# A two-layer graph convolution with residual and layer norm: unrolled chunks, pairs of 1024 nodes, layer 2 in node layout, row statistics two at a time

## What is computed

```python
def conv(x, src, dst, ea, W_msg, W_edge, W_root, b):
    msg = x[src] @ W_msg + ea @ W_edge
    agg = segment_max(msg, dst, num_segments=N)      # -inf becomes 0
    return agg + x @ W_root + b
c1 = leaky_relu(conv(x,  ..., W1_msg, W1_edge, W1_root, b1))
c2 = leaky_relu(conv(c1, ..., W2_msg, W2_edge, W2_root, b2))
out = layernorm(x + c2)                              # over the 96 features, eps 1e-5
```

## Time and profile before

| | us |
|---|---|
| median of 3 runs | 1723.3 (1714.0 to 1755.0) |
| span of the profiled execution | 1697.5 |
| its PE, DVE, ACT, POOL busy | 979, 1044, 667, 1056 |
| its stage A, to the last scan of layer 1 | 760 |
| its stage S, to the first scan of layer 2 | 340 |
| its stage B | 598 |

### The profile page before, as it was taken

The page is one execution under the profiler, slowest core; times in us unless marked ns, Lnnn a source line. Parts: engine busy times, 40 slices in busy tenths (PEclk is TensorE's granted clock), DMA queues, the critical chain, the costliest instruction groups (busy, mean ns, idle before and its releaser), DMA issues.

```text
span 1697.5 us, 21367 instructions
## 1 busy us (share of the span) xinstructions
PE 978.8 (58%) x3038; PEld 438.7 (26%) x3038; DVE 1044.2 (62%) x3881; ACT 666.9 (39%) x1717; POOL 1055.8 (62%) x1182
## 2 busy tenths in 40 slices
PE   3476866666666465687778778454343443334441
PEld 1233433233333232332322223222111111111210
DVE  2356666555555465679999999665544555445553
ACT  1345654444444354568888888400000000000000
POOL 5566656455545545617877767666667766677665
PEclk9678877778777777889999999755655655556555
DMA  6366756556555455755444444533333333233320
GB/s 172 93 183 207 240 178 181 174 175 194 175 177 184 146 179 171 220 177 185 157 153 154 152 146 154 164 111 106 104 95 94 107 99 104 79 102 99 107 74 21
DMA packets 142053, 245.87 MB, mean 145 GB/s; under 512 B 31470, under 2 KB 70120, under 8 KB 142022
## 3 DMA queue, kind: packets, MB, share of 16 engines
q1 hardware_dynamic: 103462, 161.26, 30.4%
q0 software_dynamic: 31360, 45.90, 11.5%
q10 hardware_dynamic: 7200, 38.40, 6.0%
HBM read 122.70 MB, written 125.07 MB: 146 GB/s over the span
## 4 chain that ended last, share of the span: by engine, by line
issue 34%; DVE 15%; PE 15%; another core or an unknown queue 15%; ACT 11%; POOL 4%; DMA 1%; DVEq 1%; ACTq 1%; POOLq 1%
ACT ob L686 5%; PE ps L529 5%; PE ps_r L529 4%; DVE stat L820 3%; PE ps_t L519 2%; POOL out L302 2%; PE ps_m L529 2%; DVE c1t L780 2%; DVE mv L831 2%; ACT c2t L647 2%; POOL g_src L295 2%; DVE c2t L780 2%; DVE stage L923 1%; DVE mx L790 1%
## 5 line engine op out<-in xcount | busy, mean ns | idle before, releaser
L686 ACT ACTIVATE ob<-ps_y,shift,rstd 128x96 f32<-128x96 f32 x784 | 273.7, 432 | 139.9 <-DVE shift L859 71.4
L820 DVE BATCH_NORM_STATS2 stat<-ps_y 128x6 f32<-128x96 f32 x784 | 147.0, 248 | 192.4 <-remote 141.1
L302 POOL DMA_INDIRECT agg_table<-stage,now_end x196 | 221.2, 1128 | 68.5 <-issue 68.2
L302 POOL DMA_INDIRECT out<-stage,now_end x196 | 200.4, 1022 | 60.0 <-issue 59.1
L295 POOL DMA_INDIRECT g_src<-in_x,now_gat x196 | 195.8, 999 | 63.0 <-issue 62.9
L295 POOL DMA_INDIRECT g_dst<-in_x,now_gat x196 | 195.2, 996 | 59.7 <-issue 59.1
L529 PE MATMUL ps<-xtb,wr 97*96 97x512 f32 x392 | 224.1, 655 | 11.0 <-ACT c1t L647 2.9
L295 POOL DMA_INDIRECT g_src<-agg_table,now_gat x196 | 196.8, 1004 | 52.9 <-issue 52.6
L529 PE MATMUL ps<-c1t,wr 97*96 97x512 f32 x392 | 212.4, 625 | 11.5 <-issue 10.3
L519 PE MATMUL ps_t<-ident,g_src 128*96 128x128 f32 x392 | 90.2, 374 | 209.9 <-DMA g_src<-agg_table,now_gat 176.7
L655 ACT ACTIVATE std<-mv,epsc 128x4 f32<-128x4 f32 x245 | 74.6, 305 | 296.5 <-issue 185.5
(11 more groups left out here) (54 smaller groups left out, 1494.3 us busy)
## 6 DMA issues: line engine op xcount, KB each, us to landing
xtb<-in_xt SPq DMA_DIRECT2D x196, 192.0 KB
agg_table<-zero ACTq DMA_DIRECT2D x50, 750.0 KB
out<-ob SPq DMA_DIRECT2D x195, 192.0 KB
mask<-mask_row SPq DMA_DIRECT2D x98, 192.0 KB
xd_keep<-g_dst SPq DMA_DIRECT2D x49, 192.0 KB
root_keep<-rt SPq DMA_DIRECT2D x49, 192.0 KB
c1d_keep<-c1d SPq DMA_DIRECT2D x49, 192.0 KB
rt<-root_keep SPq DMA_DIRECT2D x49, 192.0 KB
```

What stands on the lines that cost most here:

```text
L302: nc.gpsimd.indirect_dma_start(out=rows, out_offset=bass.IndirectOffsetOnAxis(ap=now_end[:, e.slot(R), r:r + 1], axis=0), in_=stage[:, e.s ...
L686: last = nc.scalar.activation(ob[:, d.slot(R), row(r)], ps_y[k][:, row(r)], ACT.Identity, bias=shift[:, k, r:r + 1], scale=rstd[:, k, r:r ...
L820: last = V.bn_stats(stat[:, k, r, :], rows(r))
```

## The change

The kernel is written anew around the same stages; the mathematics of the edges stays.

- **Unrolled.** No hardware loop is left. Every semaphore target, address and index column is a constant. The index copies on POOL go; the indirect DMAs take their indices from the full tables. Stage A and the dense work are 98 ticks (49 with a chunk), stage B is 49 steps.
- **Pairs.** Dense work goes by pairs of 1024 nodes (NQ = 98), one a tick: the layer-1 product in two halves into a two-bank ps_1, and one ACTIVATE over 96x1024.
- **Layer 2 in node layout.** Leaky(z) is written as 0.01 z + 0.99 relu(z). ACT applies relu straight out of PSUM. Layer 2 is c1t.T @ (0.99 W2r) + x.T @ (0.01 W1r W2r), a sum of two products that come out nodes-by-features, since the activations are now the stationary operand: 8 pieces of 128 nodes, two products each. `w12` is made once at the start. The transposes back go. x is loaded a second time in node layout (xn). After it ACT writes 0.99 relu(z) to yo, DVE adds 0.01 z + x (`dense_u`) and sums (`dense_y`).
- **Statistics.** One BATCH_NORM_STATS2 reads two rows interleaved (`two_rows`), so that its two halves are the statistics of one row each; the aggregation goes. The variance is a sum, and ACT divides by 96 inside the square root.
- **Norm.** Four of a pair's eight rows per partition are normalized by DVE (`tensor_scalar` in place), four by ACT.
- **Edges.** The own rows (g_dst) of a chunk are transposed one tick later than the sources. keep_own is issued in the chunk's own tick. In stage A nothing is copied to `stage`: the scatters read `nat`. In stage B the product of c1d and the transposition of the maxima (as a product with the identity) accumulate in one PSUM bank (`sums_back`), and LAG is 4. The scatters of stage S follow one another with no wait but that for the chunk's maxima.

```diff
-LAG = 3
+J = 8
+PN = P * J
+NQ = -(-N // PN)
+XR = 4
+YR = 4
+LAG = 4
...
+        c1t = sb("c1t", [D, 2, PN])
+        yo = sb("yo", [P, YR, J * D])
...
+        ps_1 = pb("ps_1", [P, 2, CH])
+        ps_z = pb("ps_z", [P, 2, CH])
...
+            for c in range(NCH):
+                k = c % R
+                if c >= R:
+                    pool.wait_ge(a_t, c - R + 1)
+                gather(x, src_i, c, g_src, k, l_src)
+                if c >= R:
+                    pool.wait_ge(a_own, c - R + 1)
+                    pool.wait_ge(k_xd[k], 16 * turn(c, R))
+                gather(x, own_i, c, g_dst, k, l_dst)
             pool.wait_ge(s_cleared, 16 * NZ)
...
+            for c in range(NCH):
+                pool.wait_ge(a_nc, c + 1)
+                scatter(table, c, sc_t)
+            pool.wait_ge(sc_t, 64 * NCH)
...
+            for t in range(TICKS):
+                if t + 1 < NCH:
+                    load_edges(t + 1, t + 1, a_r, a_scan)
+                load_pair(t + 2)
+                if t < NCH:
+                    keep_own(t)
+                if 2 <= t < NCH + 2:
+                    keep(t - 2)
+                store_pair(t - 3)
...
+            def layer2(q):
...
+                pe.wait_ge(d_c1, q + 1)
+                if q >= 1:
+                    pe.wait_ge(d_c2, q)
+                    pe.wait_ge(d_u, q)
+                for j in range(J):
+                    nc.tensor.matmul(ps_z[:, j // 4, row(j % 4)], c1t[:, q % 2, cols(j)], w2s[:, :],
+                                     start=True, stop=False)
+                    last = nc.tensor.matmul(ps_z[:, j // 4, row(j % 4)], xtb[:, q % XR, cols(j)], w12[:, :],
+                                            start=False, stop=True)
+                last.then_inc(d_2, 1)
...
+            for t in range(TICKS + 1):
+                c, o = t, t - 1
+                if c < NCH:
...
+                    forward(g_src[:, k, :], a_t)
+                layer2(t - 1)
+                if 0 <= o < NCH:
...
+                    forward(g_dst[:, ko, :], a_own)
+                layer1(t)
+                if c < NCH:
...
+                    product(ps_m, wm1[:, :], xe[:, k, :], a_m)
...
+                    product(ps_r, wr1[0:D, :], xe[0:D, k, :], a_r)
+                if 0 <= o < NCH:
+                    maxima_back(o)
+                    pe.wait_ge(a_xd, o + 1)
+                    pe.wait_ge(a_rc, min(c + 1, NCH))
...
+                    product(ps_r, wr1[0:D, :], xd[:, o % 2, :], a_r1)
...
+            for t in range(TICKS + 3):
+                c, o = t, t - 1
+                dense_std(t - 2)
+                if c < NCH:
...
+                    copy(xe[0:D, k, :], ps_t[0:D, :], a_xe)
+                    clear(c)
+                dense_c2(t - 1)
+                if 0 <= o < NCH:
...
+                    copy(xd[:, o % 2, :], ps_t[0:D, :], a_xd)
+                dense_c1(t)
+                dense_norm(t - 2)
+                if c < NCH:
...
+                    copy(rt1[:, k, :], ps_r[0:D, :], a_rc)
...
+            for t in range(TICKS + 3):
+                c, o = t, t - 1
+                dense_u(t - 1)
+                dense_rstd(t - 2)
+                dense_y(t - 1)
+                dense_shift(t - 2)
+                dense_stats(t - 1)
+                dense_norm(t - 2)
```

More of the change, by code:

```diff
@@ L48 @@
 NZ = N * D // (P * ZCOL)
[L49 to L110, removed]
+assert N * D % (P * ZCOL) == 0 and NZ == NCH + 1 and NQ == 2 * NCH and (N - (NQ - 1) * PN) % J == 0
 def gnn_kernel(nc, x, xt, src, dst, dst_next, dst_row, dst_prev, eat,
@@ L197, in gnn_kernel @@
         ps_n = pb("ps_n", [P, CH])
-        ps_1 = pb("ps_1", [P, CH])
-        ps_2 = pb("ps_2", [P, CH])
-        ps_y = [pb(f"ps_y{k}", [P, CH]) for k in range(2)]
         s_const = sem("s_const")
@@ L512, in _, with forward @@
             pe.wait_ge(s_ident, 1)
-            pe.wait_ge(s_const, 10 * 16)
+            pe.wait_ge(s_const, 9 * 16)
             pe.wait_ge(s_ones, 2)
-            def forward(ps, rows, done):
-                for r in range(TPC):
-                    last = nc.tensor.transpose(ps[0:D, cols(r)], rows[:, row(r)], ident[:, :])
-                last.then_inc(done, 1)
-            def back(ps, t, done):
-                for r in range(TPC):
-                    last = nc.tensor.transpose(ps[:, row(r)], t[:, cols(r)], ident[0:D, 0:D])
+            nc.tensor.transpose(ps_t[0:D, 0:D + 1], wr1[:, :], ident[0:D + 1, 0:D + 1]).then_inc(w_t, 1)
+            pe.wait_ge(w_tc, 1)
+            nc.tensor.matmul(ps_m[0:D + 1, 0:D], w1t[:, :], wr2[0:D, :], start=True, stop=True).then_inc(w_p, 1)
+            pe.wait_ge(w_12, 2)
+            def forward(rows, done):
+                for r in range(TPC):
+                    last = nc.tensor.transpose(ps_t[0:D, cols(r)], rows[:, row(r)], ident[:, :])
                 last.then_inc(done, 1)
@@ L633, in _ @@
-            each_chunk(pe, step_b)
-            sums_back(LAST_CHUNK)
+                k = c % R
+                pe.wait_ge(l_c1d[k], 16 * turn(c, R) + 16)
+                pe.wait_ge(b_scan, c + 1)
+                if c >= 1:
+                    pe.wait_ge(b_nc, c)
+                    pe.wait_ge(e_u, c)
+                for r in range(TPC):
+                    nc.tensor.matmul(ps_n[:, row(r)], c1d[:, k, cols(r)], wr2[:, :], start=True, stop=False)
+                    last = nc.tensor.matmul(ps_n[:, row(r)], mx2[:, c % 2, cols(r)], ident[0:D, 0:D],
+                                            start=False, stop=True)
@@ new lines, in dense_norm @@
+            def dense_norm(q):
+                if not 0 <= q < NQ:
+                    return
+                act.wait_ge(d_shift, q + 1)
+                for j in range(4, J):
+                    last = nc.scalar.activation(yo[:, q % YR, row(j)], yo[:, q % YR, row(j)], ACT.Identity,
+                                                bias=shift[:, q % 2, j:j + 1], scale=rstd[:, q % 2, j:j + 1])
+                last.then_inc(d_done_a, 1)
+            act.wait_ge(w_t, 1)
+            copy(w1t[:, :], ps_t[0:D, 0:D + 1], w_tc)
```

935 lines of the change are left out of this document (388 added, 547 removed).

## The result

The changed kernel takes 2072.8 us (2070.7 to 2074.8) where the kernel before takes 1727.4 (1714.0 to 1755.0): 1.206 of before, interval 1.200 to 1.213. Forecast were 1563 us, with 1440 to 1710 as the range and 0.13 for slower. Its profiled span is 2071.5 us.

A forecast was written before the change was run, and what follows sets the result against it. Bound by stages: POOL's back-to-back issue delaying PE's completions in A and B, DVE in S. 1697.5 less 81 (A), 55 (S), 24 (B) gave a 1537.5 us span; plus 26 to the median, 1563, range 1440 to 1710.

The follow-up runs named there:

- the version at 0.964: Changed kernel with scatters waiting for PE's layer 2, one extra wide product a tick and, in stage S alone, layer 1 ahead of layer 2: 1368.9 us for 1421.1.

## What to carry to other kernels

Count PE's instructions, not its time, wherever POOL issues indirect DMAs back to back for longer than a few of them: if the trace of before shows ACT or DVE idle by "remote" under such runs, each PE instruction may cost 1.4 us there, as here, and short products with a weight load each are the worst that can be put beside them. Where a stage is made of many short products, look at the granted clock of the stage and not at the busy share, and try one wide product a tick in a bubble of PE: 0.86 us of unused work took 5 us off each tick here. Run the kernel before beside every candidate, since the same program took 1411 us in one hour and 1755 in another.

## What was not expected of the hardware

- Under POOL's gapless run, in late hours, a dense tick takes 1.40 to 1.41 us for each of PE's instructions: 24, 72 and 80 of them in 33.6, 101.6 and 112.7 us. That can also be 2.8 us for each pass. In clean hours the same run delays nothing. What differs between the hours is open.
- PE busy for 388.75 of 390 us stays at half clock, 0.51, with 32 of its 36 passes a tick of 96 columns. One product of 512 columns in each tick keeps it at 1.00.
- The clock held for 1 to 12 ticks of S at PE 83% busy before it fell (17 with a push of sixteen wide products between them). After that it came back for single ticks only (9.7 us instead of 11.7), and once, with layer 1 first, for four ticks of 5.8 to 7.2.
- A scatter's issue of 0.97 us becomes 1.56 beside a DVE sum of two SBUF tensors, and stays 0.97 beside `tensor_scalar` (S of the version at 0.964).
